# Local attention on one core: queries normalised on GpSimd before they are transposed, the row minimum as the exponential's bias

## The reference, cut to what matters

```python
h = shift_token(x)
q, k, v = split(h @ wqkv)                      # 8 heads of 64
q = l2norm(q) * qs;  k = l2norm(k) * ksc       # l2norm over the 64 of a head
q, k = rotary_xpos(q, k)
sim = (8.0 * q) @ k.T                          # 128 queries of a window, 256 keys: its own and the window before
sim = where(mask, -big, sim)
out = softmax(sim) @ v
x = x + out @ wo
```

## Time and profile before

| | |
|---|---|
| median of 3 runs | 1051.81 us (1051.48 to 1053.34) |
| profiled execution, its own time | 1053.46 us |
| its span, first to last instruction | 1051.7 us |
| granted TensorE clock, mean | 0.979 |
| PE busy | 973.0 us, 93% |
| PEld busy | 766.9 us, 73% |
| DVE busy | 698.1 us, 66% |
| ACT busy | 556.3 us, 53% |
| POOL busy | 396.0 us, 38% |

### The profile page before, as it was taken

How to read it: one execution, slowest core, us unless ns; L and a number is a source line. 1 busy time by engine, 2 the same in 40 slices (tenths; PEclk the granted TensorE clock), 3 DMA queues, 4 the chain that set the end, 5 groups by cost and what they waited for, 6 DMA issues and landing times.

```text
span 1051.7 us, 17917 instructions
## 1 busy us (share of the span) xinstructions
PE 973.0 (93%) x5656; PEld 766.9 (73%) x5656; DVE 698.1 (66%) x1814; ACT 556.3 (53%) x1217; POOL 396.0 (38%) x416
## 2 busy tenths in 40 slices
PE   5889969999999988999999789998999999979987
PEld 4668855777676866777777568887777777758876
DVE  6878477366575677777777555665777777745563
ACT  4567731403031326777777644454777777754432
POOL 4232513113130356666665310006565656520030
PEclk9899989999999999999999999999999999989999
DMA  7101012000000000000001020000000000000002
GB/s 245 67 1 60 20 41 105 1 1 0 0 0 1 1 21 2 2 22 0 21 0 31 12 97 15 4 25 1 2 22 0 21 0 21 17 12 18 9 2 84
DMA packets 15174, 26.34 MB, mean 25 GB/s; under 512 B 1098, under 2 KB 11712, under 8 KB 14352
## 3 DMA queue, kind: packets, MB, share of 16 engines
q1 hardware_dynamic: 15120, 25.68, 7.4%
HBM read 20.53 MB, written 2.10 MB: 22 GB/s over the span
## 4 chain that ended last, share of the span: by engine, by line
PE 71%; DVE 11%; issue 6%; ACT 4%; POOL 4%; SPq 2%; DMA 1%; POOLq 0%; DVEq 0%; ACTq 0%
PE bank L1534 31%; PE bank L1729 5%; PE bank L1823 5%; PE bank L1681 5%; PE bank L1850 4%; PE bank L1835 4%; PE bank L1869 4%; PE bank L1802 2%; SPq L332 1%; PE bank L1861 1%; PE bank L1692 1%; PE bank L1809 1%; DVE scores L981 1%; POOL scanned L399 1%; PE bank L1600 1%
## 5 line engine op out<-in xcount | busy, mean ns | idle before, releaser
L1396 ACT ACTIVATE probs<-scores,row_bias,q_rnorm 128x256 f32<-128x256 f32 (+1 forms) x256 | 143.7, 565 | 10.8 <-DVE row_bias L987 10.3
L981 DVE CUSTOM_DVE_ANT_0 scores<-bank,mask 128x256 f32<-128x256 f32 (+1 forms) x256 | 89.3, 385 | 22.1 <-PE bank L1823 17.7
L530 POOL TENSOR_TENSOR norms<-norms,minus_half 128x16 f32<-128x16 f32 x32 | 93.6, 2924 | 2.7
L1534 PE MATMUL bank<-wqkv_hi,x_hi 128*128 128x512 f32 x192 | 85.5, 445 | 1.8 <-ACT v_tok L1373 0.8
L513 POOL TENSOR_TENSOR k_tok<-rot 128x512 f32<-128x512 f32 x32 | 41.2, 1287 | 100.1 <-DVE rot L955 100.1
L1534 PE MATMUL bank<-wqkv_lo,x_hi 128*128 128x512 f32 x192 | 77.3, 403 | 0.0
L1534 PE MATMUL bank<-wqkv_hi,x_lo 128*128 128x512 f32 x192 | 77.3, 402 | 0.0
L1823 PE MATMUL bank<-k_t,q_t 64*128 64x256 f32 (+1 forms) x512 | 67.6, 383 | 10.1 <-DVE row_max L981 8.6
L1835 PE MATMUL bank<-ident,probs 128*128 128x128 f32 x448 | 67.2, 280 | 5.2 <-ACT probs L1396 5.0
L1128 DVE SCALAR_TENSOR_TENSOR hidden<-bank,lcols,hidden 128x512 f32<-128x512 f32 (+1 forms) x48 | 36.0, 749 | 53.7 <-PE bank L1534 29.4
L1368 ACT ACTIVATE squares<-bank 128x512 f32<-128x512 f32 x64 | 38.3, 598 | 59.1 <-PE bank L1534 59.1
(11 more groups left out here) (236 smaller groups left out, 2584.3 us busy)
## 6 DMA issues: line engine op xcount, KB each, us to landing
w_stage<-in_wm_l_dram SPq DMA_DIRECT2D x8, 534.0 KB, 3.6
w_stage<-in_wqkv_dram SPq DMA_DIRECT2D x2, 1536.0 KB, 7.1
out_dram<-stream SPq DMA_DIRECT2D x4, 512.0 KB, 3.7
emb<-in_ctx_dram SPq DMA_DIRECT2D x1, 1536.0 KB, 6.7
inner<-in_w_gate_dram SPq DMA_DIRECT2D x1, 1152.0 KB, 10.3
stream<-in_x_dram SPq DMA_DIRECT2D x2, 512.0 KB, 5.8
stream<-in_x_dram SPq DMA_DIRECT2D x1, 1024.0 KB, 12.7
ew<-in_pos_bias_dram SPq DMA_DIRECT2D x1, 1024.0 KB, 11.3
```

Source lines behind the costliest of these rows:

```text
L530: pool.tensor_tensor(norms[:, 2, :], norms[:, 1, :], minus_half[:, :], ALU.pow).then_inc(c_rn, 1)
L981: dve.tensor_tensor_reduce(scores[:, i % 2, e, 0:nk], bank[6 + e][:, (i % 2) * 2 * P:(i % 2) * 2 * P + nk], mask[:, 2 * P - nk:2 * P], 1.0 ...
L1396: act.activation(probs[:, i % 2, e, 0:nk], scores[:, i % 2, e, 0:nk], ACT.Exp, bias=row_bias[:, w % 2, h:h + 1], scale=q_rnorm[:, w, h:h + 1],
L1534: ins = pe.matmul(out, stationary, moving, start=(first and i == 0), stop=(last and i == len(terms) - 1))
```

## The change

The norms' factor is put to the queries: `rnorm` ends with a product on GpSimd of the whole `q_tok` of the tile (128x512) with the factor of each head, in place of the small product that made `q_rnorm`. The eight and a minus sign go into the queries' rope tables, so the scores come out negated and complete. The mask is now +1e30, VectorE takes the minimum of the row in place of the maximum, and this minimum is the exponential's bias as it is; its scale is the constant -1. `q_rnorm`, `row_bias` and the instruction L987 with its two waits are gone. `transpose_q` on TensorE waits for the product as well. Nothing is moved in any queue.

```diff
-NEG = -1e30
+FAR = 1e30
@@ tiles
-        q_rnorm = sb("q_rnorm", [P, 4, HEADS])
-        row_max = sb("row_max", [P, 2, HEADS])
-        row_bias = sb("row_bias", [P, 2, HEADS])
+        row_min = sb("row_min", [P, 2, HEADS])
@@ def rnorm(n, par) on GpSimd (par is the tile's buffer, n % 2)
                 if not (isinstance(n, int) and n == 0):
                     wait_alone(pool, c_kn, n)
+                    wait_alone(pool, c_rq, n)
                 pool.tensor_scalar(norms[:, 1, :], norms[:, 0, :], 1e-24, 1.0, ALU.max, ALU.mult).then_inc(c_clip, 1)
                 pool.wait_ge(c_clip, n + 1)
                 pool.tensor_tensor(norms[:, 2, :], norms[:, 1, :], minus_half[:, :], ALU.pow).then_inc(c_rn, 1)
                 wait_alone(pool, c_rn, n + 1)
-                pool.tensor_scalar(q_rnorm[:, w, :], norms[:, 2, 0:HEADS], QK_SCALE, 0.0, ALU.mult, ALU.add)\
+                wait_alone(pool, c_add, 2 * n + 1)
+                q = q_tok[:, par, :].rearrange("p (h d) -> p h d", d=DH)
+                pool.tensor_tensor(q, q, norms[:, 2, 0:HEADS].unsqueeze(2).to_broadcast([P, HEADS, DH]), ALU.mult)\
                     .then_inc(c_rq, 1)
@@ def tables(l) on VectorE
+                    sign = (-QK_SCALE, 1.0)[i // 2]
...
-                        dve.tensor_tensor(dst, src, s.to_broadcast([P, TT, DH]), ALU.mult).then_inc(c_tab, 1)
+                        dve.scalar_tensor_tensor(dst, src, sign, s.to_broadcast([P, TT, DH]), ALU.mult, ALU.mult)\
+                            .then_inc(c_tab, 1)
@@ def masked(n, w, i) on VectorE
-                                             mask[:, 2 * P - nk:2 * P], 1.0, NEG, ALU.add, ALU.max,
-                                             row_max[:, w % 2, 2 * i + e:2 * i + e + 1]).then_inc(c_tt, 1)
-                dve.wait_ge(c_tt, 2 * u + 2)
-                dve.wait_ge(c_rq, n + 1)
-                dve.scalar_tensor_tensor(row_bias[:, w % 2, 2 * i:2 * i + 2], row_max[:, w % 2, 2 * i:2 * i + 2],
-                                         -1.0, q_rnorm[:, w, 2 * i:2 * i + 2], ALU.mult, ALU.mult).then_inc(c_nb, 1)
+                                             mask[:, 2 * P - nk:2 * P], 1.0, FAR, ALU.add, ALU.min,
+                                             row_min[:, w % 2, 2 * i + e:2 * i + e + 1]).then_inc(c_tt, 1)
@@ def exps(n, w, i) on ScalarE
-                act.wait_ge(c_nb, u + 1)
+                act.wait_ge(c_tt, 2 * u + 2)
...
-                                   bias=row_bias[:, w % 2, h:h + 1], scale=q_rnorm[:, w, h:h + 1],
+                                   bias=row_min[:, w % 2, h:h + 1], scale=-1.0,
@@ def transpose_q(n, par) on TensorE
                 pe.wait_ge(c_kt, n + 1)
+                pe.wait_ge(c_rq, n + 1)
```

More of the change, by code:

```diff
@@ L231, in build @@
         (c_zero, c_tab, c_xs, c_xt, c_xt_out, c_p, c_sq, c_v, c_ss, c_clip, c_rn, c_rq, c_rope, c_add,
-         c_kn, c_t, c_kt, c_qt, c_qk, c_tt, c_nb, c_ex, c_pt, c_pt_out, c_pv, c_ri, c_rb, c_rt, c_rt_out, c_ot_out,
+         c_kn, c_t, c_kt, c_qt, c_qk, c_tt, c_ex, c_pt, c_pt_out, c_pv, c_ri, c_rb, c_rt, c_rt_out, c_ot_out,
          c_wo, c_res) = signals(
             "c_zero c_tab c_xs c_xt c_xt_out c_p c_sq c_v c_ss c_clip c_rn c_rq c_rope c_add c_kn c_t "
-            "c_kt c_qt c_qk c_tt c_nb c_ex c_pt c_pt_out c_pv c_ri c_rb c_rt c_rt_out c_ot_out c_wo c_res")
+            "c_kt c_qt c_qk c_tt c_ex c_pt c_pt_out c_pv c_ri c_rb c_rt c_rt_out c_ot_out c_wo c_res")
         (d_shift, d_stats, d_aggr, d_eps, d_rstd, d_norm, d_tp, d_tp_out, d_w1, d_gelu, d_act, d_w2, d_res0) = signals(
@@ L369, in _ @@
                                pattern=[[-1, P]], channel_multiplier=1).then_inc(ready_consts, 1)
-            pool.affine_select(out=mask[:, :], in_=mask[:, :], compare_op=ALU.is_ge, fill=NEG, base=P,
+            pool.affine_select(out=mask[:, :], in_=mask[:, :], compare_op=ALU.is_ge, fill=FAR, base=P,
                                pattern=[[-1, 2 * P]], channel_multiplier=1).then_inc(pool_ready, 1)
             pool.wait_ge(pool_ready, 6)
-            pool.affine_select(out=mask[:, :], in_=mask[:, :], compare_op=ALU.is_ge, fill=NEG, base=0,
+            pool.affine_select(out=mask[:, :], in_=mask[:, :], compare_op=ALU.is_ge, fill=FAR, base=0,
                                pattern=[[1, 2 * P]], channel_multiplier=-1).then_inc(ready_consts, 1)
@@ L521, in spread_sums, with rnorm @@
                     .then_inc(c_rb, 1)
-            def rnorm(n, w):
+            def rnorm(n, par):
                 pool.wait_ge(c_ss, n + 1)
@@ L568, in window @@
                 if two:
-                    rnorm(n + 2, (w + 2) % TT)
+                    rnorm(n + 2, w % 2)
                 if w:
@@ L936, in tables @@
                         for lo, other in ((0, DH // 2), (DH // 2, 0)):
-                            dve.tensor_tensor(dst[:, :, lo:lo + DH // 2], src[:, :, lo:lo + DH // 2],
-                                              s[:, :, other:other + DH // 2].to_broadcast([P, TT, DH // 2]),
-                                              ALU.mult).then_inc(c_tab, 1)
-                    else:
-                        dve.tensor_tensor(dst, src, s.to_broadcast([P, TT, DH]), ALU.mult).then_inc(c_tab, 1)
+                            dve.scalar_tensor_tensor(dst[:, :, lo:lo + DH // 2], src[:, :, lo:lo + DH // 2], sign,
+                                                     s[:, :, other:other + DH // 2].to_broadcast([P, TT, DH // 2]),
+                                                     ALU.mult, ALU.mult).then_inc(c_tab, 1)
+                    else:
+                        dve.scalar_tensor_tensor(dst, src, sign, s.to_broadcast([P, TT, DH]), ALU.mult, ALU.mult)\
+                            .then_inc(c_tab, 1)
             def rope_products(n, w, i):
```

## The result

The changed kernel took 1045.86 us (median of 8 runs, 1044.14 to 1049.35), the kernel before 1051.75 us in the same series; the ratio is 0.9942, 95% interval [0.9926, 0.9959]. I had said 1049.0 us, a gain of 2.8 us; it was 5.9 us, about the number of rival 1. Two later series of the changed kernel gave 1046.31 us (0.9948 [0.9931, 0.9965]) and 1048.74 us (0.9973 [0.9958, 0.9988]). Over all 30 timed runs of the changed kernel the mean is 1047.3 us, over 141 of the kernel before 1051.8 us: 4.4 us. Two executions that took about twice as long, one of the kernel before (1924.74 us) and one of fill6_before (2442.79 us), are in no figure here. The later series ran on five chips, so a ratio, which compares a kernel with the kernel before in the same series, says more than a median set beside one of another series. The size of the gain is not a fixed number, and why is most of what follows.

The account below looks back on a forecast made before the run. PE was taken as the bound in middle windows, so gains come only where PE waits. Terms -2.0 - 0.7 - 0.35 - 0.2 + 0.5 = -2.75 us took the median from 1051.81 to 1049.0 us; range 1045.8 to 1051.8.

Parts of the forecast that it names:

- rival 1: Last windows: shorter gaps keep TensorE's clock up, each tail gains 1.6 us more, 1045.8 us in all; chance 0.14.
- two tails: Last windows of both layers: shorter chain of scores, L981 and exponentials gives 1.0 us each, together -2.0 us.
- batch boundaries and middle: Six batch boundaries: L1802 waits less for residual L1008, 0.12 us each, -0.7 us; middle windows unchanged.
- start of layer 1: L1835 at 729.93 waits for the fourth exponential, which comes earlier: -0.35 us.
- start of layer 0: Second scores wait for one L987 less, -0.2 us; POOL's product colliding with norm_keys adds 0.5 us.
- low clock in the tails: Last windows: the forecast's own sum had no term for a changed clock.
- 1.82 us of idle time shrink only by about 0.2: Argument against the clock staying up: TensorE's idle time in the last window shrinks only by about 0.2 us.
- the step: Removal of DVE's small L987 between L981 and the exponential, taken as 0.2 us a step.
- the scale: Exponential L1396 with a constant scale, taken as 87 ns shorter, 592 to about 505 ns; if free, tails give only -0.5 each.
- The collision: Start of layer 0: POOL's product and DVE's norm_keys, released together, shut each other out, +0.5 us.
- Rival 2: Next to nothing: exponential's pace doesn't fall with the scale, POOL wins at the start; -0.7 us, 1051.1 us; chance 0.16.
- rival 3: Slower: POOL's product is long (3 us) and shuts out norm_keys; +2.75 us, 1054.6 us; chance 0.10.

Follow-up runs that it names:

- fill6_before: Kernel before with six extra identity matmuls ahead of the second scores of each layer's last window; 1050.41 us, ratio 0.9973.
- shift_320: Kernel before with an unused tile of 320 bytes per partition behind row_bias, moving later tiles; 1052.59 us, ratio 1.0014.
- gap_after: Changed kernel with one extra DVE product ahead of the second scores' minima in each layer's last window; 1050.08 us, ratio 0.9978.
- the two fillers: Kernel before with twelve or six extra identity matmuls ahead of the last window's second scores; 1050.58 us (0.9993) and 1050.41 us (0.9973).
- The pad: Changed kernel with an unused 192 bytes per partition behind row_min, restoring old tile addresses; 1048.15 us (0.9971), again 1047.98 us (0.9955).
- scale_place: Changed kernel with the exponential's scale (-1) read from a tile in 16 unused bytes behind rstd, no other tile moved; 1052.57 us, ratio 1.0003.

## Why the prediction was wrong

Undisturbed stages give the change this sum, beside my terms:

| place | forecast | measured | from |
|---|---|---|---|
| two tails | -2.0 | -3.06 | 35.28 to 33.75 |
| batch boundaries and middle | -0.7 | -0.75, of it -0.6 by placement | 159.96 to 159.59, twice |
| start of layer 1 | -0.35 | -0.37 | two waits, 0.82 to 0.64 and 0.52 to 0.33 |
| start of layer 0 | +0.3 | +0.3 | attention's first matmul to first projection: 43.58, 43.51, 43.67 (shift_320) to 44.00, 43.72, 43.99 |
| placement, behind layer 0's attention | none | +1.4 | 132.70 to 133.69 without start of layer 1 |
| low clock in the tails | 0 | -1.2 | at the MLP's first matmul: 0.6 a tail in 12, none in 18 |

Without the clock that is about -2.5 us against my -2.75. That it is so near is luck: the tails gave 1.1 us more, and placement in the middles 0.6, while the boundaries gave 0.5 less and placement took 1.4. With the clock the sum is -3.7 us, and the pooled runs gave -4.4. That the first series landed on rival 1's 1045.8 us is luck as well: the clock in the tails gave 1.2 us of its 3.2.

**The step that failed** is the one behind rival 1: "1.82 us of idle time shrink only by about 0.2", so the clock would stay low there, chance 0.14. The gap shrank by 0.24 us, as forecast, and behind it the clock stayed up. Over the profiled tails: in 14 tails with a gap of 1.82 or 1.92 us the stretch behind it was low in 6; in 22 tails with 1.58 us, in none; with the gap filled, in none of 4. The second place in a tail, behind the waits for the last exponentials and for `o_t`, was low in 9 of the 14 and 3 of the 22, but it cost next to nothing. gap_after (a longer gap, more lost clock) and the two fillers (no gap, less) support the gap as a cause, in both directions; that is one profile of each, with lost clock from 11 or 12 timed runs. The gap doesn't decide alone: the same 1.82 us let the clock fall or not. My rival had 1.6 us for each tail, every time; where the first place was low it cost 1.4 to 1.6, and the mean is 0.6, since that came in a part of the tails.

**The other steps.** The tails gave 1.53 us each and not 1.0: the step was right (0.48 measured, about 0.4 forecast), the scale was mis-sized (1.13 against 0.5). I let the shorter exponentials count in window w = 2 and once at the end, and gave them nothing in w = 3; the stages show 0.47 us for them in w = 2, 0.48 in w = 3 and 0.18 behind. Boundaries: about 0.1 us a layer for the change itself (159.67 in shift_320, 159.59 after), not 0.35. The collision came as written: the first transposition of keys starts 17.41 to 17.42 us behind the attention's first matmul in the three profiles of the old kernel and 17.82 or 17.83 us after the change, 0.4 us later (forecast 0.5); in part that comes back in a shorter wait for the row extremes (2.88 to 2.98 us against 3.08). Rival 2 fell with the exponential's 501 ns, rival 3 with the product's 1.05 us. What I had no term for at all is the placement.

**What stays open.** The first series' 5.9 us holds some 2 us that neither stages nor tails carry, the pooled 4.4 us some 0.7. Three series of one kernel from 1045.86 to 1048.74 us show how far one series can be off. The pad's median is open as told, and scale_place's is the strongest thing against this account: with the gap at 1.58 us and both tails free of the costly low stretch it is as slow as the kernel before.

## What to carry to other kernels

Near the end of a stage, where TensorE idles between short bursts, a few tenths of a microsecond of gap can be worth several times their length in clock (here 0.24 us of gap, and 0.6 us a tail on the mean), and a handful of idle matmuls in the gap can test it. A low stretch in which TensorE waits anyway costs nothing: follow it to the next stage before booking it. A change that drops or adds a small tile moves all tiles behind it: put a pad in its place before comparing, or a strided DMA's new price is booked on the wrong edit. Where whole runs scatter by 5 us, compare the periods between like instructions: they repeat to 0.02 us.

## What the runs showed that I had not expected

- A strided DMA of rows of 512 bytes between SBUF tiles occupies its queue 11.27 or 12.04 us by the destination's place in 512 bytes (416; 224 or 288), 10.98 us where both ends begin at a multiple.
- GpSimd's product of 128x512 with an operand spread over 64 columns takes 1.05 us, less than the plain sum of the same size, 1.29 us.
- A low stretch of TensorE's clock behind the waits for the last exponentials lengthened the last period by up to 0.8 us and moved the MLP's first matmul by 0.17 at most.
- Six extra matmul calls in TensorE's gap made the kernel before faster, 0.9973 [0.9955, 0.999].
